# The first transfers in another order, and the empty rows of both expert tables written in eight pieces

## The chip, the core and the metric

The kernel runs on one core of one Trainium2 chip. The core has five engines that run their own instruction streams and meet at semaphores: TensorE (PE, matrix products), VectorE (DVE), ScalarE (ACT), GpSimd (POOL) and SyncE (SP), which here computes nothing and issues nearly all transfers. The metric is the device time of one execution in microseconds (us); lower is better.

## What is computed

The reference is a stack of four residual blocks on x, which is 16 batches of 128 tokens with 128 features, with a condition vector and a context of 77 rows for each batch:

```python
x = x + xcond_0(layernorm(x), cond, ctx)   # adaLN, self-attention, cross-attention, GLU feed-forward
x = x + ffn_0(layernorm(x))                # shared expert + 7 routed experts, top 2
x = x + xcond_1(cond, ctx, layernorm(x))   # slot attention over ctx, 3 rounds
x = x + ffn_1(layernorm(x))                # 8 routed experts, top 1
```

The first block is the one that matters here. For each batch it does

```python
h1 = adaln(x, t, norm1_w, norm1_b);  x = mha(h1, h1, wq, wk, wv, wo) + x        # 16 heads of 64
h2 = adaln(x, t, norm2_w, norm2_b);  x = mha(h2, context, wq2, wk2, wv2, wo2) + x
h3 = adaln(x, t, norm3_w, norm3_b);  x = glu_ff(h3, w1, b1, w2, b2) + x
```

## The kernel before, in words

All arithmetic is float32. The first phase is a software pipeline over the 16 batches, written out by hand for every engine (`iteration(i, S)`, from i = -1 to 17). In iteration i the self-attention of batch i ("A"), the cross-attention of batch i-1 ("B") and the feed-forward and routing of batch i-2 ("C") stand interleaved in twelve steps, with the q, k and v projections of batch i+1 ("N"). The tables `FILL`, `SCORE_STEP`, `SUM_STEP` and `TURN_STEP` set the order within an iteration; each engine executes its stream strictly as written, with waits on semaphores in between.

Before the pipeline come the loads. SP issues them in the order of the code, all on one queue, and the engines wait for them by semaphore:

- `ld_x_first` and `ld_small`: the first two batches of x, condition, adaLN weights, identity, columns (lines 485 to 489).
- `ld_att1` (48): wq, wk, wv of self-attention (line 491), waited for by PE before iteration -1.
- `ld_x`: the other 14 batches of x (line 492, in `load_x` at line 483), waited for by DVE in iteration 0, where the early norms of batches 2 to 5 begin.
- `ld_rows` (48): the row constants, spread to all partitions, the output weights `wo[0]` of self-attention, and the router weights `wr`. POOL waits for all three before it adds a bias row to x (`add_row`, line 1832), and PE before `wo1` of iteration 0 (line 642).
- `ld_ctx`: the context, which PE transposes (line 609) before iteration 0.
- `ld_att2` (64): the q and k weights of cross-attention (`qk2_w`, line 498), its v weights `wv[1]` (line 499) and its output weights `wo[1]` (line 500). PE waits for all four at its first use of any, `v2_0` of iteration 0 (line 633), then makes the products `a2_0` to `a2_3` (line 711).
- `ld_ff`, `ld_moe`, `ld_slot`: what later phases use.

In iteration 0 PE's stream begins with the first two score units of batch 0 (line 652), then `v2_0`, `a2_0`, `a2_1`, `a2_2`, the next two score units (line 652), `q1_1` (line 627) and the transposes of the first softmax (line 677). ACT empties `v2_0` (line 1045) before its first exponential (line 1118); DVE's sums and POOL's scaling (line 1881) follow from that exponential.

The values of cross-attention go through DRAM: SP stores a block of 128 context rows when ACT has emptied it (`store_values`, line 514) and loads the 77 rows of one batch when they are stored and the buffer is free (`load_values`, line 520). `values(i)` does both for batch i. The load for batch b is used by PE at line 689 in iteration b+1, second half.

Two tables in DRAM, `rows_a` (118 regions of 128 rows) and `rows_b` (135 regions), receive the tokens that go to the experts. Their empty rows are written first, by copies of prepared arrays from DRAM to DRAM (line 531), after `values(0)`. POOL waits for `zeroed` before its first scatter of a token row into `rows_a`, in iteration 14.

After the first phase come the shared expert, the routed blocks of table a, slot attention, and the blocks of table b. None of that code is touched.

Of the kernel before, what the change touches and what calls it, by code (L numbers as in the profile page):

```python
# [11 lines left out]
P = 128  # L12
B = 16
# [65 lines left out]
FIRST_TILES = 2  # L79
# [2 lines left out]
LN_STEPS = 3  # L82

SCATTER_FROM = 4

RANK_AT = [last + 3 for _, last in PARTS["a"][:-1]]

# [129 lines left out]
def at(i, count):  # L217

    return count(i)
# [17 lines left out]
def program(nc, A, row_names, out):  # L237
    PLAN = proj_plan()
    with ExitStack() as ctx:
# [9 lines left out]
        def sem(name):  # L249
            return ctx.enter_context(nc.semaphore(name))  # L250
# [133 lines left out]
        def quads(t):  # L384
# [6 lines left out]

        ld_x, ld_small, ld_att1, ld_att2, ld_ff, ld_ctx = (
            sem(n) for n in ("ld_x", "ld_small", "ld_att1", "ld_att2", "ld_ff", "ld_ctx"))
        ld_x_first, ld_rows, rows_added = sem("ld_x_first"), sem("ld_rows"), sem("rows_added")
        pre_dve = sem("pre_dve")
        pre_ada = sem("pre_ada")
# [84 lines left out]
        def _(sp):  # L481
            def load_x(first, last, sem_):
                sp.dma_start(x_sb[:, first:last, :], A["x"][first:last].rearrange("b s d -> s b d")).then_inc(sem_, 16)
# [5 lines left out]
            sp.dma_start(cols[:, :], A["cols"]).then_inc(ld_small, 16)  # L489
            for j in range(3):  # L490
                sp.dma_start(watt[:, 0, j, :], A["att_w"][j]).then_inc(ld_att1, 16)
            load_x(FIRST_TILES, B, ld_x)
            sp.dma_start(rows[:, :], A["rows"].partition_broadcast(P)).then_inc(ld_rows, 16)
            sp.dma_start(ctx_n[:, :, :], A["ctx"].rearrange("b c d -> c b d")).then_inc(ld_ctx, 16)
            sp.dma_start(wo[0], A["att_wo"][0].rearrange("(c p) n -> p c n", p=P)).then_inc(ld_rows, 16)
            sp.dma_start(wr[:, :], A["wr_t"]).then_inc(ld_rows, 16)
            for j in range(2):
                sp.dma_start(qk2_w[:, j, :, :], A["att2_qk"][j].rearrange("(c p) n -> p c n", p=P)).then_inc(ld_att2, 16)
            sp.dma_start(wv[1], A["att_w"][3]).then_inc(ld_att2, 16)
            sp.dma_start(wo[1], A["att_wo"][1].rearrange("(c p) n -> p c n", p=P)).then_inc(ld_att2, 16)  # L500
            sp.dma_start(w1[:, :], A["ff_w1"]).then_inc(ld_ff, 16)
            sp.dma_start(w2[:, :, :], A["ff_w2"].rearrange("(c p) n -> p c n", p=P)).then_inc(ld_ff, 16)
            sp.dma_start(gate_up[:, :], A["gate_up"][EA]).then_inc(ld_moe, 16)
# [21 lines left out]
                    store_values(i)  # L525
                load_values(i)

            values(0)
            sp.wait_ge(consts_ready, 1)
            for t, pad in ((rows_a, A["pad_a"]), (rows_b, A["pad_b"])):  # L530
                sp.dma_start(*(v.rearrange("(p n) d -> p (n d)", p=P) for v in (t, pad))).then_inc(zeroed, 16)
            for i in range(1, B):
                values(i)
            first_phase_over(sp)
            sp.dma_start(cb2[:, :, :].rearrange("p b d -> p (b d)"),
                         A["cond"].rearrange("b d -> (b d)").partition_broadcast(P)).then_inc(ld_cond, 16)
# [58 lines left out]
        def _(pe):  # L595
# [102 lines left out]
            def fill(i, name):  # L698
                half = int(name[-1]) if name[-1] in "01" and "_" in name else 0
                if STREAM[name] == "N" and i == -1:  # L700
                    pe.wait_ge(pre_act, 1)
                if STREAM[name] == "N" and i + 1 in [first for first, _ in X_GROUPS]:
                    emptied_by([first for first, _ in X_GROUPS].index(i + 1), "hT")
                if name.startswith("a2"):
                    if name == "a2_0":
                        pe.wait_ge(ld_att2, 64)
                    t, j = use(i, name), int(name[-1])
                    p = slice(DH * (j % 2), DH * (j % 2) + DH)
                    for h in range(QH):
                        c = 4 * (j // 2) + h  # L710
                        mm = pe.matmul(t[:, h * P:(h + 1) * P], qk2_w[p, 1, c, :], qk2_w[p, 0, c, :], start=True, stop=True)
                    mm.then_inc(proj_full, 1)
                if name.startswith("g2"):
                    if i == 0:
                        emptied_by(i, "a2_3")
                    b, t = i - i % 2, use(i, name)
                    for n, h in enumerate(G2_HEADS[int(name[-1])]):
                        mm = pe.matmul(t[:, n * 2 * C:(n + 1) * 2 * C], a2[:, h, :], ctxT[:, b * C:(b + 2) * C],  # L718
                                       start=True, stop=True)
                    mm.then_inc(proj_full, 1)  # L720
                if name.startswith("v2"):
                    if i == 0:
                        pe.wait_ge(ld_att2, 64)
                    rows_ = slice(P * V2_BLOCK[i], min(P * V2_BLOCK[i] + P, B * C))
                    v_proj(i, name, wv[1], ctxT[:, rows_], half, rows_.stop - rows_.start)
                if name.startswith("q1"):
                    qk_proj(i, name, wq, h1T[:, i + 1, :], half, P)
                if name.startswith("k1"):
                    qk_proj(i, name, wk, h1T[:, i + 1, :], half, P)
                if name.startswith("v1"):  # L730
                    v_proj(i, name, wv[0], h1T[:, i + 1, :], half, P)
                if name == "wo1":
                    if i == 0:
                        pe.wait_ge(ld_rows, 48)
                    pe.wait_ge(o_kept, at(i, lambda t: units_before(t) // 2 + QH // 2))
                    o_proj(i, name, "A", wo[0])
                if name == "wo2":
                    pe.wait_ge(o_kept, at(i, lambda t: units_before(t) // 2))
                    o_proj(i, name, "B", wo[1])
                if name == "hT":  # L740
                    first, last = X_GROUPS[i]
                    t = use(i, name)
                    pe.wait_ge(pre_dve, x_normed(i))
                    for b in range(first, last):
                        mm = pe.transpose(t[:, (b - first) * P:(b - first + 1) * P], z_all[:, b, :], eye[:, :])
                    mm.then_inc(proj_full, 1)
                if name == "h2T":
                    pe.wait_ge(z_ready["A"], i)
                    turn(i, name, zA)
                if name == "h3T":  # L750
                    pe.wait_ge(z_ready["B"], i - 1)
                    turn(i, name, zB)
                if name == "gate":
                    if is_iteration(i, 2):
                        pe.wait_ge(ld_ff, 32)
                    emptied_by(i, "h3T")
                    qk_proj(i, name, w1[:, FF:2 * FF], h3T[:, :], 0, P)
                if name == "lin":
                    qk_proj(i, name, w1[:, 0:FF], h3T[:, :], 0, P)
                if name == "ffout":  # L760
                    t = use(i, name)
                    emptied_by(i, "lin")
                    for c in range(FF // P):
                        mm = pe.matmul(t[:, 0:D], glu[:, c, :], w2[:, c, :], start=(c == 0), stop=(c == FF // P - 1))
                    mm.then_inc(proj_full, 1)
                if name == "zT":
                    pe.wait_ge(z_ready["C"], i - 1)
                    turn(i, name, zC)
                if name == "rank":
                    rank_sums("a", RANK_AT.index(i), use(i, name))  # L770
                if name == "logit":
                    t = use(i, name)
                    emptied_by(i, "zT")
                    pe.matmul(t[:, 0:EA], zT[:, :], wr[:, :], start=True, stop=True).then_inc(proj_full, 1)
# [1032 lines left out]
        def _(pool):  # L1807
# [47 lines left out]
            def early_scatter(i, k):  # L1855

                for part, rank_at in enumerate(RANK_AT):
                    first, last = PARTS["a"][part]
                    if (i, k) == (rank_at, 0):
                        pool.wait_ge(ld_slot, 48)  # L1860
                        for n in range(2):
                            pool.tensor_copy(sent[n][:, first:last, D], tok_ids[:, n, first:last]).then_inc(sent_ready, 1)
                    if (i, k) == (rank_at + 2, SCATTER_FROM):
                        pool.wait_ge(zeroed, 32)
                        pool.wait_ge(routed["a"], part + 1)
                        pool.wait_ge(sent_ready, 2 * part + 2)
                        pool.wait_ge(z_kept, last + 1)
                    n = (N_STEPS - SCATTER_FROM) * (i - rank_at - 2) + k - SCATTER_FROM
                    if k >= SCATTER_FROM and n in range(2 * (last - first)):
                        scatter_one("a", n % 2, first + n // 2)  # L1870
# [178 lines left out]
```

## Time and profile before

| | us |
|---|---|
| median of 3 runs | 942.78 |
| range of the runs | 941.45 to 943.51 |
| span of the profiled execution | 942.8 |
| PE busy in it | 803.7 (85%) |
| DVE busy | 568.8 (60%) |
| ACT busy | 540.2 (57%) |
| POOL busy | 360.0 (38%) |

The profiled execution and the median agree, so its instants can be used as they stand. The page gives busy time by engine, the span in forty slices with TensorE's granted clock, and the groups of instructions with what ended the idle time before them. Other views of the same execution are the timeline (instructions with their start and length), the waits (who waited for whom), the windows (busy time, clock and transfer rate in a stretch), the transfers with their time from issue to landing, and the chain that ended last, followed back through a stretch.

### The profile page before, as it was taken

How to read it: one execution, taken by the hardware profiler on the slowest of the kernel's cores; microseconds unless marked ns; L12 is line 12 of the kernel's file. 1: busy time of each engine (PE TensorE's matmuls, PEld its weight loads, DVE VectorE, ACT ScalarE, POOL GpSimd, SP SyncE). 2: the span in 40 equal slices, each digit the busy share in tenths (PEclk: the TensorE clock that was granted, in tenths of full speed). 3: DMA queues.
4: the chain of work that ended last, by engine and by line, in shares of the span. 5: the costliest groups of instructions: out<-in, count | busy, mean ns of one | idle time of the engine just before them, and what ended most of it. 6: DMA issues, size and time to landing. Idle time of an engine off the chain costs nothing.

```text
span 942.8 us, 18988 instructions
## 1 busy us (share of the span) xinstructions
PE 803.7 (85%) x6173; PEld 673.0 (71%) x6173; DVE 568.8 (60%) x1941; ACT 540.2 (57%) x1147; POOL 360.0 (38%) x559
## 2 busy tenths in 40 slices
PE   5899899999999999999987588999978786861693
PEld 5777787888878888788876456999746565651693
DVE  2576887677866668776575352333558787885012
ACT  2565676667766677666754222333448888851362
POOL 1233454333333333332656150566422222226363
PEclk9897999999999999999998789999855979795697
DMA  9699111001010101000100131888600000001574
GB/s 284 230 314 342 70 37 37 15 1 50 2 37 1 51 1 37 15 1 37 48 27 20 45 105 40 245 249 243 209 7 1 1 0 1 1 1 37 152 208 126
DMA packets 43275, 78.50 MB, mean 83 GB/s; under 512 B 5339, under 2 KB 28587, under 8 KB 42651
## 3 DMA queue, kind: packets, MB, share of 16 engines
q1 hardware_dynamic: 39691, 70.09, 23.8%
q0 software_dynamic: 3488, 7.20, 2.2%
q8 instruction: 52, 0.85, 0.4%
q14 instruction: 44, 0.36, 0.1%
HBM read 63.98 MB, written 30.13 MB: 100 GB/s over the span
## 4 chain that ended last, share of the span: by engine, by line
PE 55%; DVE 20%; issue 9%; POOL 6%; ACT 6%; DMA 2%; SPq 2%; DVEq 0%; ACTq 0%; POOLq 0%
PE bank L899 5%; PE bank L627 5%; PE bank L689 5%; PE bank L652 4%; PE bank L642 3%; DVE sb_smax L1396 3%; PE bank L633 3%; PE bank L677 3%; DVE sb_row_sum L1406 3%; PE bank L907 3%; PE bank L661 3%; PE bank L1008 2%; PE bank L1016 2%; DVE sb_st_all L1704 2%; PE bank L718 2%
## 5 line engine op out<-in xcount | busy, mean ns | idle before, releaser
L1881 POOL TENSOR_TENSOR sb_expd<-sb_expd,sb_rden 128x512 f32<-128x512 f32 (+1 forms) x128 | 112.4, 878 | 259.4 <-DVE sb_rden L1410 259.3
L1396 DVE TENSOR_REDUCE sb_smax<-bank 128x4 f32<-128x512 f32 (+1 forms) x128 | 74.1, 579 | 64.3 <-PE bank L652 39.7
L1973 POOL TENSOR_TENSOR sb_rstd_all<-sb_rsq_all,sb_halves 128x4 f32<-128x4 f32 x44 | 45.2, 1026 | 133.5 <-DVE sb_rsq_all L1711 133.5
L677 PE MATMUL bank<-sb_eye,sb_expd 128*128 128x128 f32 (+1 forms) x512 | 77.5, 278 | 5.7 <-POOL sb_expd L1881 5.2
L1118 ACT ACTIVATE sb_expd<-sb_shifted 128x512 f32<-128x512 f32 (+1 forms) x128 | 69.8, 545 | 18.9 <-DVE sb_shifted L1399 17.9
L677 PEld LDWEIGHTS bank<-sb_eye,sb_expd 128*128 128x128 f32 (+1 forms) x512 | 59.7, 145 | 26.8 <-issue 13.5
L1406 DVE TENSOR_REDUCE sb_row_sum<-sb_expd 128x4 f32<-128x512 f32 (+1 forms) x128 | 73.0, 570 | 9.4 <-ACT sb_expd L1118 9.4
L1112 ACT ACTIVATE sb_probT<-bank 128x512 f32<-128x512 f32 (+1 forms) x128 | 74.3, 590 | 7.2 <-PE bank L677 6.9
L1399 DVE TENSOR_TENSOR sb_shifted<-bank,sb_smax 128x512 f32<-128x512 f32 (+1 forms) x128 | 75.0, 586 | 4.4
L627 PE MATMUL bank<-sb_h1T,sb_watt 128*128 128x128 f32 x512 | 72.1, 287 | 4.7 <-DMA sb_watt<-att_w 2.3
L689 PE MATMUL bank<-sb_probT,sb_v 128*64 128x128 f32 (+1 forms) x1024 | 71.7, 283 | 5.0 <-issue 3.4
L627 PEld LDWEIGHTS bank<-sb_h1T,sb_watt 128*128 128x128 f32 x512 | 64.1, 198 | 9.5 <-DVE sb_xb L1385 3.7
L689 PEld LDWEIGHTS bank<-sb_probT,sb_v 128*64 128x64 f32 (+1 forms) x1024 | 56.1, 139 | 14.7 <-issue 4.7
L899 PE MATMUL bank<-sb_blk_xT,sb_up_w 128*128 128x128 f32 x456 | 57.1, 275 | 0.0
L1939 POOL DMA_INDIRECT back_a<-sb_blk_y,sb_dest_a x38 | 37.0, 973 | 48.7 <-issue 24.9
L899 PEld LDWEIGHTS bank<-sb_blk_xT,sb_up_w 128*128 128x128 f32 x456 | 54.0, 192 | 0.0
L1671 DVE TENSOR_TENSOR sb_hid<-bank,sb_hid 128x384 f32<-128x384 f32 x38 | 21.2, 558 | 51.1 <-ACT sb_hid L1167 51.1
L661 PE MATMUL bank<-sb_g,sb_h2T 128*128 128x308 f32 x128 | 48.4, 460 | 0.0
L1201 ACT ACTIVATE sb_z_all<-sb_S,sb_nbias,sb_rstd_all 128x128 f32<-128x128 f32 x96 | 39.3, 482 | 10.6 <-DVE sb_nbias L1717 10.3
L1167 ACT ACTIVATE sb_hid<-bank 128x384 f32<-128x384 f32 x38 | 18.6, 491 | 40.6 <-PE bank L899 40.6
L652 PE MATMUL bank<-sb_k1T,sb_q1T 64*128 64x128 f32 x512 | 38.2, 289 | 3.6 <-DVE sb_shifted L1399 3.1
L718 PEld LDWEIGHTS bank<-sb_ctxT,sb_watt 128*128 128x128 f32 x256 | 36.8, 190 | 4.6 <-issue 2.4
(256 smaller groups left out, 1917.2 us busy)
## 6 DMA issues: line engine op xcount, KB each, us to landing
sb_up_w<-gate_up SPq DMA_DIRECT2D x38, 384.0 KB
rows_b<-pad_b SPq DMA_DIRECT2D x1, 8775.0 KB, 53.6
rows_a<-pad_a SPq DMA_DIRECT2D x1, 7670.0 KB, 27.9
sb_up_w<-w1b SPq DMA_DIRECT2D x23, 256.0 KB
sb_v<-v_all SPq DMA_DIRECT2D x16, 308.0 KB
v_all<-sb_v_rows SPq DMA_DIRECT2D x9, 512.0 KB, 2.6
sb_blk_x<-rows_a SPq DMA_DIRECT2D x38, 65.0 KB, 3.3
sb_watt<-att_w SPq DMA_DIRECT2D x4, 512.0 KB, 6.3
```

What stands on the lines that cost most here:

```text
L627: mm = pe.matmul(t[:, c * n:(c + 1) * n], w[:, (4 * half + c) * P:(4 * half + c + 1) * P], src, start=True, stop=True)
L652: mm = pe.matmul(score[(u + r) % 2][:, h, :], q1T[p, 4 * (j // 2) + h, :], k1T[p, 4 * (j // 2) + h, :], start=True, stop=True)
L661: pe.matmul(score[u % 2][:, :, 0:C], h2T[:, :], g2[:, QH * j:QH * (j + 1), first:first + C], start=True, stop=True).then_inc(score_done, 1)
L677: mm = pe.transpose(trans[u % 2][0:n, h, :], expd[:, (units_before(i) + u) % EXP_RING, h, 0:n], eye[:, :])
L689: mm = pe.matmul(pvo[DH * r:DH * r + DH, h, :], v[:, 8 * (j // 2) + 2 * h + r, :], probT[0:n, (u - 1 + r) % 2, h, :], start=True, stop=True)
L899: mm = pe.matmul(bank[1 + 2 * j + v][:, c * P:(c + 1) * P], up_w[:, (u + 1) % NSLOT, (j * CA + c) * P:(j * CA + c + 1) * P], blk_xT[:, v, ...
L1112: act.activation(probT[0:n, u % 2, :, :], trans[u % 2][0:n, :, :], ACT.Copy).then_inc(probT_ready, 1)
L1118: act.activation(expd[:, (units_before(i) + u) % EXP_RING, :, 0:n], shifted[:, u % 2, :, 0:n], ACT.Exp, scale=DH ** -0.5).then_inc(exp_don ...
L1396: dve.tensor_reduce(smax[:, u % 2, :], s_in, X, ALU.max).then_inc(max_done, 1)
L1399: dve.tensor_tensor(shifted[:, u % 2, :, 0:n], s_in, smax[:, u % 2, :].unsqueeze(2).broadcast_to([P, QH, n]), ALU.subtract).then_inc(sub_d ...
L1406: dve.tensor_reduce(row_sum[:, u % 2, :], expd[:, (units_before(i) + u) % EXP_RING, :, 0:n], X, ALU.add).then_inc(row_sum_done, 1)
L1881: pool.tensor_tensor(e, e, rden[:, u % 2, :].unsqueeze(2).broadcast_to([P, QH, n]), ALU.mult).then_inc(norm_done, 1)
```

## The change

Six lines of loads change places. The context, the v weights of cross-attention and its q and k weights now follow the self-attention weights at once; the row constants, `wo[0]` and `wr` come after them, then the 14 batches of x. The output weights `wo[1]` get a semaphore of their own, `ld_wo2`, and PE waits for that at `wo2` of iteration 2; the two waits for `ld_att2` count 48 instead of 64. The empty rows of the tables are no longer written by two copies after `values(0)`, but by eight pairs of copies, one pair after each of `values(1)` to `values(8)`. POOL's wait for `zeroed` counts 256 instead of 32.

```diff
+PAD_PARTS = 8
...
+        ld_wo2 = sem("ld_wo2")
...
             for j in range(3):
                 sp.dma_start(watt[:, 0, j, :], A["att_w"][j]).then_inc(ld_att1, 16)
-            load_x(FIRST_TILES, B, ld_x)
+            sp.dma_start(ctx_n[:, :, :], A["ctx"].rearrange("b c d -> c b d")).then_inc(ld_ctx, 16)
+            sp.dma_start(wv[1], A["att_w"][3]).then_inc(ld_att2, 16)
+            for j in range(2):
+                sp.dma_start(qk2_w[:, j, :, :], A["att2_qk"][j].rearrange("(c p) n -> p c n", p=P)).then_inc(ld_att2, 16)
             sp.dma_start(rows[:, :], A["rows"].partition_broadcast(P)).then_inc(ld_rows, 16)
-            sp.dma_start(ctx_n[:, :, :], A["ctx"].rearrange("b c d -> c b d")).then_inc(ld_ctx, 16)
             sp.dma_start(wo[0], A["att_wo"][0].rearrange("(c p) n -> p c n", p=P)).then_inc(ld_rows, 16)
             sp.dma_start(wr[:, :], A["wr_t"]).then_inc(ld_rows, 16)
-            for j in range(2):
-                sp.dma_start(qk2_w[:, j, :, :], A["att2_qk"][j].rearrange("(c p) n -> p c n", p=P)).then_inc(ld_att2, 16)
-            sp.dma_start(wv[1], A["att_w"][3]).then_inc(ld_att2, 16)
-            sp.dma_start(wo[1], A["att_wo"][1].rearrange("(c p) n -> p c n", p=P)).then_inc(ld_att2, 16)
+            load_x(FIRST_TILES, B, ld_x)
+            sp.dma_start(wo[1], A["att_wo"][1].rearrange("(c p) n -> p c n", p=P)).then_inc(ld_wo2, 16)
...
-            values(0)
-            sp.wait_ge(consts_ready, 1)
-            for t, pad in ((rows_a, A["pad_a"]), (rows_b, A["pad_b"])):
-                sp.dma_start(*(v.rearrange("(p n) d -> p (n d)", p=P) for v in (t, pad))).then_inc(zeroed, 16)
-            for i in range(1, B):
+            def empty_rows(n):
+                for t, pad, x in ((rows_a, A["pad_a"], "a"), (rows_b, A["pad_b"], "b")):
+                    each = -(-NREG[x] // PAD_PARTS)
+                    part = slice(P * each * n, P * min(each * (n + 1), NREG[x]))
+                    sp.dma_start(*(v[part, :].rearrange("(p n) d -> p (n d)", p=P) for v in (t, pad))).then_inc(zeroed, 16)
+
+            for i in range(B):
                 values(i)
+                if 1 <= i <= PAD_PARTS:
+                    empty_rows(i - 1)
...
-                        pe.wait_ge(ld_att2, 64)
+                        pe.wait_ge(ld_att2, 48)
...
+                    if is_iteration(i, 2):
+                        pe.wait_ge(ld_wo2, 16)
...
-                        pool.wait_ge(zeroed, 32)
+                        pool.wait_ge(zeroed, 32 * PAD_PARTS)
```

On SP, the first loads. Before, from the self-attention weights to the feed-forward's (`att_wo` stands twice, for `wo[0]` and then for `wo[1]`; `sb_g2<-att2_qk` is `qk2_w`, which shares its tile):

```order
L491 DMA sb_watt<-att_w 128x1024 x3
L483 DMA sb_x<-x 128x14x128
L493 DMA sb_rows<-rows 128x1245
L494 DMA sb_ctx<-ctx 77x16x128
L495 DMA sb_watt<-att_wo 128x8x128
L496 DMA sb_wr<-wr_t 128x7
L498 DMA sb_g2<-att2_qk 128x8x128 x2
L499 DMA sb_watt<-att_w 128x1024
L500 DMA sb_watt<-att_wo 128x8x128
```

And now:

```order
L495 DMA sb_watt<-att_w 128x1024 x3
L496 DMA sb_ctx<-ctx 77x16x128
L497 DMA sb_watt<-att_w 128x1024
L499 DMA sb_g2<-att2_qk 128x8x128 x2
L500 DMA sb_rows<-rows 128x1245
L501 DMA sb_watt<-att_wo 128x8x128
L502 DMA sb_wr<-wr_t 128x7
L487 DMA sb_x<-x 128x14x128
L504 DMA sb_watt<-att_wo 128x8x128
```

Four transfers moved ahead of the row constants, and x moved from the first place to the last but one. `wo[1]` stands where it stood.

Further on in SP's stream, after the loads, stand the copies of the empty rows among the stores (`v2_all<-`) and loads (`sb_v2<-`) of values. Before:

```order
L514 DMA v2_all<-sb_v2_rows 128x1024 [waits proj_act]
L520 DMA sb_v2<-v2_all 77x1024 [waits v2_stored]
L531 DMA rows_a<-pad_a 128x15340 [waits consts_ready]
L531 DMA rows_b<-pad_b 144x15600
L514 DMA v2_all<-sb_v2_rows 128x1024 [waits proj_act]
L520 DMA sb_v2<-v2_all 77x1024 [waits v2_stored]
L520 DMA sb_v2<-v2_all 77x1024 [waits pv_done,v2_stored]
```

And now:

```order
L518 DMA v2_all<-sb_v2_rows 128x1024 [waits proj_act]
L524 DMA sb_v2<-v2_all 77x1024 [waits v2_stored]
L518 DMA v2_all<-sb_v2_rows 128x1024 [waits proj_act]
L524 DMA sb_v2<-v2_all 77x1024 [waits v2_stored]
L536 DMA rows_a<-pad_a 16x15600
L536 DMA rows_b<-pad_b 32x8840
L524 DMA sb_v2<-v2_all 77x1024 [waits pv_done,v2_stored]
L536 DMA rows_a<-pad_a 16x15600
L536 DMA rows_b<-pad_b 32x8840
```

The first pair of copies now stands behind the store and load for batch 1, and the next pair behind the load for batch 2; six more pairs follow in the same way. The streams of PE, DVE, ACT and POOL keep their instructions in their places.

## Rows read from the trace of the kernel before

**Rows 1.** The page: the clock granted to TensorE in forty slices of the span, tenths.

```profile
PEclk9897999999999999999998789999855979795697
```

**Rows 2.** The waits of 15 to 33 us: who waited for whom, total, times, longest.

```profile
PE bank L633 <- DMA sb_watt<-att_wo: 3.5, 1, 3.5
```

**Rows 3.** The chain of 19 to 32 us: start us, us, what.

```profile
26.02 2.07 PE bank L633 x2
28.09 2.91 PE bank L711 x23
```

**Rows 4.** The timeline of 15 to 33 us: start, us, instruction [idle before <-releaser].

```profile
19.42 0.72 POOL L1832 TENSOR_TENSOR sb_x0b<-sb_x0b,sb_rows 128x256 f32<-128x256 f32 x1 [12.28 <-DMA sb_wr<-wr_t]
...
21.41 1.16 PE L652 MATMUL bank<-sb_k1T,sb_q1T 64*128 64x128 f32 x16 [0.52 <-ACT sb_ctxT L1031]
...
24.65 0.69 DVE L1399 TENSOR_TENSOR sb_shifted<-bank,sb_smax 128x512 f32<-128x512 f32 x1
...
28.62 0.62 ACT L1118 ACTIVATE sb_expd<-sb_shifted 128x512 f32<-128x512 f32 x1
...
30.26 1.04 POOL L1881 TENSOR_TENSOR sb_expd<-sb_expd,sb_rden 128x512 f32<-128x512 f32 x1 [9.43 <-DVE sb_rden L1410]
...
32.93 0.27 PE L677 MATMUL bank<-sb_eye,sb_expd 128*128 128x128 f32 x1
```

**Rows 5.** Transfers issued in 5 to 18 us: KB each, us from issue to landing.

```profile
sb_rows<-rows SPq DMA_DIRECT2D x1, 622.5 KB, 10.7
...
sb_watt<-att_wo SPq DMA_DIRECT2D x1, 512.0 KB, 8.4
...
sb_wr<-wr_t SPq DMA_DIRECT2D x1, 3.5 KB, 6.1
...
sb_g<-att_qk SPq DMA_DIRECT2D x1, 512.0 KB, 6.4
sb_watt<-att_w SPq DMA_DIRECT2D x1, 512.0 KB, 6.6
```

**Rows 6.** Windows: stretch, length, PE busy (instructions), granted clock, DMA share, GB/s.

```profile
19.00:23.00 4.00, 2.58 (x33) 1.00 1.07 348
23.00:26.00 3.00, 0.00 (x0) 0.50 1.09 378
26.00:29.80 3.80, 3.78 (x13) 0.50 1.08 436
70.00:74.00 4.00, 2.48 (x30) 1.00 0.89 296
76.00:84.80 8.80, 8.80 (x50) 0.52 1.01 335
108.00:112.00 4.00, 2.36 (x13) 1.00 0.00 0
```

**Rows 7.** The chain at full clock, at 38 us and at 112 to 119 us.

```profile
38.91 1.06 PE bank L633 x2
...
112.60 1.02 PE bank L689 x16
...
116.68 1.78 PE bank L642 x16
```

**Rows 8.** The chain at half clock, in 74 to 90 us.

```profile
78.72 1.91 PE bank L689 x16
```

**Rows 9.** The page: the second copy of empty rows, KB, us from issue to landing.

```profile
rows_b<-pad_b SPq DMA_DIRECT2D x1, 8775.0 KB, 53.6
```

**Rows 10.** The timeline at four places: DVE's, SP's, PE's and POOL's.

```profile
38.99 0.84 DVE L1270 BATCH_NORM_STATS2 sb_st_all<-sb_x 128x6 f32<-128x128 f32 x4
...
100.18 0.73 SPq L520 DMA_DIRECT2D sb_v<-v_all  x2
...
106.56 1.09 PE L689 MATMUL bank<-sb_probT,sb_v 77*64 77x128 f32 x16 [0.53 <-issue]
...
455.49 1.20 POOL L1851 DMA_INDIRECT rows_a<-sb_sent,sb_slot  x1 [0.18 <-issue]
```

More of the change, by code:

```diff
@@ L722, in fill @@
                     if i == 0:
-                        pe.wait_ge(ld_att2, 64)
+                        pe.wait_ge(ld_att2, 48)
                     rows_ = slice(P * V2_BLOCK[i], min(P * V2_BLOCK[i] + P, B * C))
```

## Prediction

> **What bounds the kernel now.** I read the page first, for the clock: it dips twice in the first four of forty slices [rows 1]. Then the waits of the opening, since the change is there: between 15 and 33 us PE waits for one transfer, 3.5 us [rows 2], and POOL for another, 12.3 us [rows 4]. The chain says which of the two counts: it runs through PE's `v2_0` (line 633) and the 24 products at line 711 behind it [rows 3], and ahead of them through the output weights of cross-attention; POOL's wait isn't on it. PE had finished the first score units at 21.41 + 1.16 = 22.57 us [rows 4] and started `v2_0` at 26.02 [rows 3]. The other engines have nothing on the path in between: DVE is done with both shifted scores at 24.65 + 0.69 = 25.34, and ACT's first exponential at 28.62 stands behind the emptying of `v2_0` [rows 4]. So in this stretch the landing of a transfer is the bound. The rest of the first phase goes by PE, DVE and the clock, whose code the change leaves alone.
>
> **The stall goes: -3.45 us.** PE waits for 64 counts of `ld_att2`. The last of them come from `wo[1]`, which `v2_0` doesn't read. Now 48 are enough, and their three transfers stand early. When do they land? The queue is the limit, its engines being full (share 1.07 [rows 6]), and transfers land about in the order of issue. Before, 896 + 622.5 + 616 + 512 + 3.5 = 2650 KB went between the self-attention weights and the end of `wr`, which landed when POOL resumed, at 19.4 [rows 4]. Now the context, wv and qk2 are 616 + 512 + 1024 = 2152 KB. By bytes I put them between the row constants (1518.5 KB, issued at 5.11, landed at 15.8) and `wo[0]` (2646 KB, 10.57 + 8.4 = 19.0) [rows 5]: 15.8 + 3.2 x 633/1128 = 17.6 us. The bounds are 15.8 and 19.4, and both lie before 22.57, the later one by 3.2 us. So the whole wait goes: 26.02 - 22.57 = 3.45.
>
> **The clock behind the stall: 0 to -1.25 us.** The clock fell to half (1.2 of 2.4 GHz) at 23.0, 0.4 us after PE went idle, and rose at 29.8, after 3.8 us of unbroken work [rows 6]. Under it `v2_0` took 2.07, against 1.06 for the same two instructions at full clock [rows 3, 7], and the 24 products took 2.91 [rows 3]; at the full-clock rate of line 642, 1.78/16 = 0.111 each [rows 7], they take 2.67. Together 1.01 + 0.24 = 1.25. Without the stall PE works on through the instant of the fall. The trace can't say whether the clock then stays: in the 4 us ahead of the fall PE was busy for 2.58, and the change adds only 0.4. But 108 to 112 us, with 2.36 of 4, saw no fall [rows 6], so such a share doesn't force one. I take it that it stays, the fall having come once PE stood still. If it falls at 23.0 all the same, PE does the same work at half clock, and the term is near 0.
>
> The Trainium skill, "TensorE: Matmul & The Clock Gate", Part 1, says that the gate's window is free-running and doesn't reset when a kernel starts. By that rule either end of this term can come up from run to run, 938.1 or 939.3. No row here shows it, since there is one profile.
>
> **What is late next.** From 22.57 on, PE ends `v2_0` at 23.6 and the 24 products at 26.3. The second score units need DVE's second subtraction, 25.34 [rows 4], which is early by 1. ACT empties `v2_0` at 23.7 and does the exponential at 24.3; POOL then scales 4.3 us earlier than its 30.26 [rows 4], at 25.9 to 27.0. The transposes at line 677, 32.93 before [rows 4], come at 28.2 in PE's order, 1.2 us after their input. PE stays last, so the shift of 4.7 arrives whole.
>
> **Loads that moved back: 0.** The row constants, `wo[0]` and `wr` now end at 3290 KB. Before, 2650 had landed at 19.4 and 3674, through qk2, at 16.59 + 6.4 = 23.0 [rows 5], which gives 21.6. POOL adds its two rows in 1.45 us, so it is through at 23.0 and at worst at 24.5; its next work is at 25.9, and that idle time is the cover. If it were gone, POOL's first scaling would be late by what is over, with 1.2 us to spare ahead of PE. PE uses `wo[0]` only behind the transposes of 28.2. x ends where wv ended, with the same bytes ahead of it: 17.88 + 6.6 = 24.5 [rows 5]; DVE first reads it at 38.99 [rows 10], some 34 now. `wo[1]` stands in its old place, landed at 26.0 [rows 3], and is used in iteration 2, behind 78.7 [rows 8]. PE's new wait costs nothing.
>
> **The empty rows in pieces: 0.** Before, 16.4 MB stood in the queue from 45 us on, and the second copy took 53.6 us to land [rows 9], at 99. The store of values for batch 1 sat behind them, so the load went out only at 100.18 [rows 10]. PE used it at 106.56, and its idle 0.53 there ends 0.1 us after ACT's last turned probabilities [rows 10]; the load wasn't late. So the pieces win nothing on the chain. Nor would the load have become late through the opening's gain, since the copies start behind `values(0)` and move with it. SP now issues 16 copies at 0.6 to 0.7 us each in an idle stream, each pair behind the load of `values(i)`. What is queued behind the last pieces is the next store of values, and at the rate of before a pair takes 53.6/8 = 6.7 us, against 13 us or more to the next thing that SP issues. The last pair goes out near 275 us; POOL asks for `zeroed` just before 455.5 [rows 10].
>
> **The sum.** 942.8 - 3.45 - 1.25 = **938.1 us**, made against the profiled execution, whose span equals the median.
>
> **The rivals.** *The clock falls at 23.0 anyway.* Only the stall goes: 942.8 - 3.45 = 939.3. For it speaks that PE's share before the instant, 2.58 of 4, is about that before the other fall, 2.48 of 4 at 70 to 74 us [rows 6].
>
> *The second dip goes as well.* From 74 to 85 us the clock is at half while PE is busy throughout, 8.8 of 8.8 us in 76 to 84.8 [rows 6]. Line 689 took 1.91 there against 1.02 at full clock [rows 7, 8], a factor of 1.87; 8.8 - 8.8/1.87 = 4.1 us, so 934.0. Against it: the thin stretch before that fall is made by DVE's instructions of iteration 1, which move along with everything else.
>
> *A new dip.* All that follows moves by 4.7 us, and a thin stretch such as 108 to 112 us may meet a fall where it met none. Priced as the second dip, one gives 938.1 + 4.1 = 942.2, no change. Two give 946.3; slower begins between the two.
>
> *The pieces land too late.* The copies have 16 and 32 rows now, 128 and 144 before. Should so few rows be carried by few of the 16 engines, a pair takes longer: with one engine 16 x 6.7 = 107 us, and eight of them from 60 us on end at 916, 460 us past POOL's wait, so 1400 us. It decides from (455 - 60)/8 = 49 us a pair, which is 2 engines or fewer. For it speaks only the new shape; against it, that there are as many rows as engines and that a row is as long as one of before (15600 elements).
>
> The Trainium skill, "DMA: Bandwidth & Descriptors", section on why a DMA increments its semaphore by 16, says that such a transfer goes over the largest number of engines, up to 16, that divides its slowest dimension. By that rule the pieces use all 16 and take the 6.7 us.
>
> **Chances.** Forecast, 938.1: 0.40. Fall at 23.0 anyway, 939.3: 0.22. Second dip gone, with or without the first, about 934.0: 0.22. One new dip, 942.2: 0.10. Slower, by two dips or late pieces: 0.06. The runs spread by 1 us to either side of the median, and so does each case. The range must leave out no more than 2 in 10: 933.3 to 941.0 holds the first two cases whole, some five sixths of the third and a tenth of the fourth, 0.40 + 0.22 + 0.18 + 0.01 = 0.81. A difference of 0.2%, 1.9 us, is about what a measurement of this kernel can tell from none. Below 940.9 lie the first three cases and a little of the fourth: 0.85. Within 0.2%: 0.09. Slower: 0.06.
>
> **What would show it.** PE goes from line 652 to `v2_0` at 22.6 without a wait for a transfer; POOL's `add_row` stands near 21.6, the transposes at line 677 near 28.2, and everything to 70 us is 4.7 us early. The clock at 23 us tells the forecast from the first rival, and the clock between 70 and 85 the second. Stores of values land within 3 us, and pairs of copies in 7. The forecast is wrong if `ld_att2` is still waited for after 22.6, if ACT or POOL becomes the late input of line 677, or if the gain of the opening is there at 70 us and is gone at 943.

## The result and the profile after

| | before | after |
|---|---|---|
| median, us | 943.14 (6 runs) | 936.44 (6 runs) |
| range, us | 941.45 to 947.19 | 932.87 to 938.01 |
| profiled execution: time, span | -, 942.8 | 932.87, 931.1 |

The ratio of after to before is 0.9916, with a 95% interval of 0.9891 to 0.9940: 7.9 us faster, by the interval between 5.7 and 10.3. The forecast was 938.1, in a range of 933.3 to 941.0. The profiled execution of after happens to be the fastest of its six, 3.6 us below their median, so its span says less than where in it the time went.

**The opening.** The chain of waits of the changed kernel, 21 to 29 us (start us, us, what). Its lines 617, 635, 641, 660, 685 and 719 are 609, 627, 633, 652, 677 and 711 of before.

```profile
21.61 1.16 PE bank L660 x16
22.78 1.05 PE bank L641 x2
23.83 2.08 PE bank L719 x23
...
26.02 0.89 PE bank L660 x15
26.92 1.09 PE bank L635 x8
28.01 0.44 PE bank L685 x4
```

No transfer stands in it any more. PE goes from the score units (line 660) to `v2_0` (line 641) at 22.78, where it stood still until 26.02 before [rows 3]; there `v2_0` takes 1.05 and not 2.07, the first 23 of the 24 instructions at line 719 take 2.08 and not 2.91 [rows 3], and the transposes come at 27.84 instead of 32.93 [rows 4] (the chain, which shows only what PE did last, has them from 28.01). The timeline shows what the prediction named beside PE: POOL's `add_row`, and its first scaling.

```profile
22.18 0.72 POOL L1842 TENSOR_TENSOR sb_x0b<-sb_x0b,sb_rows 128x256 f32<-128x256 f32 x1 [14.91 <-DMA sb_wr<-wr_t]
...
26.43 1.04 POOL L1891 TENSOR_TENSOR sb_expd<-sb_expd,sb_rden 128x512 f32<-128x512 f32 x1 [2.84 <-DVE sb_rden L1420]
...
27.84 0.60 PE L685 MATMUL bank<-sb_eye,sb_expd 128*128 128x128 f32 x4
```

**The clock.** The page's row of the clock in forty slices, and windows of the changed kernel (stretch, length, busy us and instructions of PE, PE's weight loads, DVE, ACT and POOL, granted clock, DMA share, GB/s).

```profile
PEclk9999999999999999999998689999956979795797
```

```profile
22.70:26.00 3.30, 3.30 (x33) 2.54 (x33) 3.13 (x5) 2.13 (x4) 0.89 (x2) 1.00 1.07 334
70.00:74.00 4.00, 3.34 (x35) 2.31 (x36) 1.09 (x5) 3.17 (x7) 1.68 (x3) 1.00 0.02 4
76.00:84.80 8.80, 7.94 (x79) 7.07 (x78) 7.24 (x17) 5.78 (x11) 3.33 (x4) 1.00 0.39 158
100.00:104.80 4.80, 3.77 (x13) 2.29 (x15) 2.76 (x12) 2.76 (x8) 2.59 (x6) 0.64 0.00 0
```

Both dips of the first slices [rows 1] are gone: the clock is 1.00 where it was 0.50 and 0.52 [rows 6]. A short new one, 3.4 us at half clock from 101.2, is in the last window. The copies of empty rows land in 6.4 and 8.5 us each, the stores of values in 2.6, by the page:

```profile
rows_b<-pad_b SPq DMA_DIRECT2D x7, 1105.0 KB, 8.5
rows_a<-pad_a SPq DMA_DIRECT2D x7, 975.0 KB, 6.4
...
v_all<-sb_v_rows SPq DMA_DIRECT2D x9, 512.0 KB, 2.6
```

**How much earlier, and where.** I matched PE's instructions in two traces and took the difference of their starts. The changed kernel runs 5.1 us ahead of before at 40 and 70 us, 8.2 at 97, 7.8 from 135 to 670, and 11.9 at 920. So the opening gives 5.1, the missing second dip 3.1, the stretch with the new one takes 0.4, and the last phase, whose code is the same, gives 4.1. What of this belongs to the change, and what to the one execution that was profiled, is what the experiments are for.

### The profile page after: what moved, and what is told of

The parts are those of the page before. It is cut to its first block, busy times and chain, and to the rows that moved or that the text cites. A ratio compares the mean times of both kernels' runs of the same rounds, so it can differ in the third digit from the quotient of the medians.

```text
span 931.1 us, 19002 instructions
## 1 busy us (share of the span) xinstructions
PE 796.0 (85%) x6173; PEld 666.3 (72%) x6173; DVE 568.6 (61%) x1941; ACT 540.7 (58%) x1147; POOL 360.9 (39%) x559
## 4 chain that ended last, share of the span: by engine, by line
PE 56%; DVE 21%; issue 8%; ACT 6%; POOL 6%; DMA 2%; DVEq 0%; SPq 0%; ACTq 0%; POOLq 0%
PE bank L635 6%; PE bank L909 5%; PE bank L697 5%; PE bank L660 4%; PE bank L650 3%; DVE sb_smax L1406 3%; PE bank L641 3%; PE bank L685 3%; PE bank L669 3%; PE bank L917 3%; DVE sb_row_sum L1416 3%; PE bank L1018 2%; DVE sb_st_all L1714 2%; PE bank L726 2%; PE bank L1026 2%
## 5 line engine op out<-in xcount | busy, mean ns | idle before, releaser
L1211 ACT ACTIVATE sb_z_all<-sb_S,sb_nbias,sb_rstd_all 128x128 f32<-128x128 f32 x96 | 39.3, 481 | 10.8 <-DVE sb_nbias L1727 10.4
```

## The experiments

The same lead over the first profile of before, in us, at the instants 40, 97, 135 and 920 of that profile (negative: later). "New" and "old" loads are those of after and of before. The ratio is to runs of the kernel before on the same chip.

| kernel | median us (runs) | ratio, 95% interval | lead at 40 | 97 | 135 | 920 |
|---|---|---|---|---|---|---|
| after | 936.44 (6) | 0.9916 [0.9891, 0.9940] | 5.1 | 8.2 | 7.8 | 11.9 |
| e6: after again | 934.48 (6) | 0.9892 [0.9866, 0.9919] | 5.0 | 8.2 | 8.2 | 11.4 |
| e5: before again | 946.38 (12) | 1.0009 [0.9986, 1.0031] | -2.2 | 0.9 | -0.8 | 1.1 |
| e1: new loads alone | 937.58 (5) | 0.9896 [0.9871, 0.9921] | 5.9 | 9.1 | 7.4 | 5.1 |
| e10: the same again | 940.34 (5) | 0.9900 [0.9863, 0.9938] | 5.8 | 8.9 | 4.8 | 4.4 |
| e2: pieces alone | 942.04 (9) | 0.9953 [0.9930, 0.9976] | -2.3 | 0.9 | 0.5 | 5.0 |
| e7: the same again | 944.05 (12) | 0.9996 [0.9973, 1.0019] | -2.2 | 1.0 | 1.0 | 0.3 |
| e3: old order, `wo[1]` apart | 941.97 (6) | 0.9926 [0.9899, 0.9953] | -1.2 | 1.4 | 1.5 | -0.6 |
| e4: before, stall filled | 945.13 (11) | 0.9986 [0.9960, 1.0012] | -1.6 | 1.0 | 1.0 | -1.0 |
| e9: after, stall put back | 943.64 (7) | 0.9958 [0.9932, 0.9984] | -2.4 | 0.2 | 0.2 | 0.8 |
| e11: that stall filled | 939.79 (6) | 0.9934 [0.9910, 0.9959] | 1.4 | 4.5 | 4.5 | 8.1 |
| e12: whole copies, later | 933.91 (6) | 0.9895 [0.9872, 0.9918] | 4.7 | 7.8 | 7.5 | 10.4 |
| e8: pieces on two engines | 1005.15 (2) | 1.0644 [1.0598, 1.0690] | 4.5 | 7.7 | 7.7 | -62.5 |

### The two parts alone

New loads alone (e1) is the changed kernel with the two whole copies in their old place; pieces alone (e2) is its complement. e1 against after:

```diff
...
-            for i in range(B):
+            values(0)
+            sp.wait_ge(consts_ready, 1)
+            for t, pad in ((rows_a, A["pad_a"]), (rows_b, A["pad_b"])):
+                sp.dma_start(*(v.rearrange("(p n) d -> p (n d)", p=P) for v in (t, pad))).then_inc(zeroed, 16)
+            for i in range(1, B):
                 values(i)
-                if 1 <= i <= PAD_PARTS:
-                    empty_rows(i - 1)
...
-                        pool.wait_ge(zeroed, 32 * PAD_PARTS)
+                        pool.wait_ge(zeroed, 32)
```

> The loads in their new order with wo[1] on its own semaphore; the empty rows as before, in two copies after values(0). Theory: the opening's gain comes from the loads alone, so the first transposes at the line that was 677 stand 5.1 us earlier than before (28.0), and the time is that of the changed kernel within 2 us, ratio 0.991 to 0.995; the value load for batch 1 still waits for the copies, lands near 98 us, and is not late by more than 1 us at its use near 98 to 101. Rival (the pieces bring part of the gain): ratio 0.996 or more, and the clock's dip near 74 us stays, since the copies' traffic stays.

> The loads as before, the empty rows in eight pairs. Theory: ratio 0.998 to 1.002, the stall at v2_0 of 3.45 us and both dips of the clock (23 and 74 us) as in the kernel before. Rival (the traffic of the copies has to do with the dip at 74 us, which is gone in the changed kernel): no dip there, ratio near 0.996.

Measured: 0.9896 and 0.9953. The loads bring the whole gain, and in the medians a little more than was expected of them (a ratio of 0.991 at the lowest). One expectation for e1 failed: the load for batch 1 came 2.5 us late for PE, not 1 at the most (more on this under "The pieces, or their place"). The pieces' ratio of 0.9953 didn't come back when the same kernel ran again (0.9996, below), so alone they are worth 0 to 0.5%.

### The old order with `wo[1]` on a semaphore of its own, and the stall filled

e3 keeps the order of the loads and only frees `v2_0` from `wo[1]`:

```diff
-            sp.dma_start(wo[1], ...).then_inc(ld_att2, 16)
+            sp.dma_start(wo[1], ...).then_inc(ld_wo2, 16)
...
-                        pe.wait_ge(ld_att2, 64)
+                        pe.wait_ge(ld_att2, 48)
...
+                    if is_iteration(i, 2):
+                        pe.wait_ge(ld_wo2, 16)
```

> Only wo[1] gets a semaphore of its own; order of the loads and the empty rows as before. PE then waits for wv alone, which landed at 24.5 us: the stall shrinks from 3.45 to 1.9 us. Theory: gain 1.5 us plus what the clock does, ratio 0.997 to 0.999. If the order were idle and the semaphore the whole effect, the ratio would be that of the changed kernel, 0.992.

The chain of e3, 19 to 34 us:

```profile
18.46 6.17 DMA sb_watt<-att_w
24.63 0.04 issue
24.68 2.07 PE bank L637 x2
26.75 3.83 PE bank L715 x23
```

wv[1] is now the late transfer, and PE waits 1.7 us by the waits. The clock falls at 23.6 all the same, now for 10.2 us, so line 715 (711 in before) takes 3.83: at 40 us this kernel is 1.2 behind the profile of before, with half of its stall gone. But its ratio, 0.9926, with an interval of 0.9899 to 0.9953, isn't the 0.997 to 0.999 of my theory; it is what I expected if the semaphore were the whole effect. The profiled execution was the slowest of the six (945.01 us, the fastest 936.34), so its trace may not stand for the others. By the traces the new order adds 6.3 us at 40 us to what the semaphore brings (5.1 against -1.2); by the medians how much it adds isn't shown.

e4 leaves the wait where it is and lets PE work in it:

```diff
+                    if i == 0 and name == "v2_0":
+                        for _ in range(7):
+                            pe.matmul(use(i, name)[:, :], eye[:, :], wq[:, 0:512], start=True, stop=True)
                     if i == 0:
                         pe.wait_ge(ld_att2, 64)
```

> The kernel before with 7 products of 128x512 put on PE ahead of v2_0 (their result is overwritten by v2_0), so that PE stands idle no more while it waits; nothing else differs. v2_0 then starts near 26.3 instead of 26.0. Theory: the clock does not fall at 23 us, v2_0 and the 24 products take 3.1 us instead of 5.0, and the transposes stand 1.5 us earlier than before; this is the clock's share of the opening's gain. Rival (the fall at 23.0 is due to what came before it): it falls all the same, and the kernel is slower by 0.3 us or more.

The chain of e4, 22 to 33 us:

```profile
23.44 6.21 PE bank L724 x14
29.65 0.86 PE bank L633 x2
30.51 2.08 PE bank L711 x23
```

The seven products took 6.21 us, not the 3.5 of the stall, and pushed `v2_0` from 26.02 to 29.65, where 26.3 was expected. But the clock stayed at full until 75 us, and of these 3.6 us only 1.6 are left at 40 us: the other 2.0 are what the kernel before loses at half clock behind its stall. The filling overshot, so the pair e9 and e11 asks the same with a shorter one.

### Before, after and the pieces again

> The kernel before, unchanged, for a second profile and for the spread of a ratio that must be 1. Theory: the dips of the clock lie elsewhere than in the first profile, since they come at instants of their own and meet the program at another place; the opening's dip lasts 6.8 or 10.2 us, the dip near 74 us lasts 0 to 10.2 us; ratio 0.998 to 1.002. Rival (the dips belong to the code): both as in the first profile.

> The changed kernel, unchanged, for a second profile. Theory: no stall at v2_0 and no dip before 30 us again, with the opening 5 to 6 us shorter than in the kernel before; the later dips lie elsewhere than in the first profile, so the gain behind 470 us is between -2 and +4 us; ratio 0.990 to 0.994. Rival (the pieces bring 3 us of it): ratio lower than that of the loads alone, 0.9896, by 0.002 or more.

> The pieces alone once more; their first ratio, 0.9953, was lower than the theory's 0.998. Theory (the pieces bring nothing, the first ratio was the clock's luck): 0.998 to 1.001, and stall and dip at 23 us as before. Rival (the pieces bring 2 to 4 us, by the clock or by transfers in 45 to 99 us): 0.993 to 0.997.

The second profile of before (e5) is the most instructive trace of all. Its chain, 19 to 34 us and 100 to 112 us:

```profile
26.15 2.08 PE bank L633 x2
28.22 3.83 PE bank L711 x23
...
104.74 3.43 DMA sb_v<-v_all
108.17 0.04 issue
108.21 1.09 PE bank L689 x16
```

Three things differ from the first. The opening dip lasts 10.2 us instead of 6.8, and the lead falls to -2.2. There is no dip at 74 us, which gives 3.1 back. And then PE waits 3.1 us for the values of batch 1, at 105, which costs 1.8 of lead. The sum is -0.8: two executions within 1 us of each other that spend their time differently. e6 repeats after within 0.4 us in every column up to 135.

### The stall put back

e9 is the changed kernel with one wait more; e11 is e9 with three products in the wait.

```diff
                     if i == 0:
                         pe.wait_ge(ld_att2, 48)
+                        pe.wait_ge(ld_wo2, 16)
```

```diff
+                    if i == 0 and name == "v2_0":
+                        for _ in range(3):
+                            pe.matmul(use(i, name)[:, :], eye[:, :], wq[:, 0:512], start=True, stop=True)
```

> The changed kernel, with one wait more: v2_0 waits for wo[1] again, as before the change. PE is ready for it at 22.7 us; wo[1] is issued at 17.2 and its landing took 7.3, so v2_0 should start at 24.5 to 25.5, a stall of 1.8 to 2.8 us. Theory (what makes the half clock of the opening is PE standing still before v2_0, not the order of the loads): the clock falls at 23 to 24 us for 6.8 to 13.7 us, the 24 products take 2.9 to 3.8 instead of 2.1, everything at 45 to 70 us is 5 to 8 us later than in the changed kernel, ratio to the kernel before 0.997 to 1.002. Rival (the fall belongs to the old order, or to chance): no fall, the lag against the changed kernel is the stall alone, 2 to 3 us, ratio 0.992 to 0.994.

> The kernel with the stall put back, and in the stall three products of 128 by 512 of the identity with wq, written into the bank that v2_0 writes over anew: 0.9 us each, so 2.7 us of work where PE would stand still. Theory (idle makes the fall): no half clock between 22 and 45 us, v2_0 at 25.4 to 26, everything at 45 to 70 us later than in the changed kernel by the 2.7 to 3 us of the delay alone, less what was slack; ratio 0.992 to 0.995, so faster than the kernel with the empty stall although v2_0 starts no earlier. Rival: the clock falls as in the empty stall, same time as that one or later.

The chain of e9, and then that of e11, 20 to 34 us:

```profile
20.77 1.16 PE bank L660 x16
21.93 3.85 issue
25.78 2.04 PE bank L641 x2
27.83 3.83 PE bank L719 x23
```

```profile
22.95 2.77 PE bank L732 x6
25.72 0.73 issue
26.45 1.10 PE bank L641 x2
27.55 2.08 PE bank L719 x23
```

The chain calls the wait of e9 "issue", without naming the transfer. With PE idle for 3.85 us the clock falls (at 24.9 us, for 10.2) and line 719 costs 3.83; at 40 us e9 is 7.5 us behind after, 3.0 of them from the later start of `v2_0`, which leaves 4.5 for work at half clock. With PE busy in the same wait `v2_0` starts 0.7 us later still, nothing runs at half clock, and at 40 us e11 is 3.7 behind after: only its later start. The ratios stand in the same order, 0.9958, 0.9934, and 0.9916 and 0.9892 without the wait, though the intervals of e9 and e11 overlap and each has one trace. So it isn't the order of the loads that holds the clock here; it is that PE doesn't stand still before `v2_0`.

One profile doesn't fit this account. In e7 the clock fell at 21.1 us, 1.7 us before PE's wait for `wo[1]` began, while PE worked on the first score units (stretch, length, PE busy and instructions, granted clock, DMA share, GB/s):

```profile
18.12:18.57 0.45, 0.00 (x0) 1.00 0.89 262
18.57:21.10 2.53, 1.76 (x18) 1.00 1.02 295
21.10:22.84 1.74, 1.74 (x16) 0.50 1.13 382
```

There the score units already take 1.94 us instead of 1.16. The 0.45 us at 18.12 is a wait for the context, which also stood behind other loads in the old order. Whether that wait brought the fall wasn't tried.

### The pieces, or their place

e10 repeats the new loads alone:

> The new order of loads with the old two copies of empty rows, a second time. Theory (the pieces are worth nothing): the same ratio as the changed kernel within the interval, 0.988 to 0.992, and no half clock ahead of 95 us. Rival (the pieces bring about 2 us by thinner traffic behind 45 us): 0.993 to 0.995.

The waits of 90 to 115 us, of e1 and then of e10 (who waited for whom, total, times, longest):

```profile
PE bank L693 <- DMA sb_v<-v_all: 2.5, 1, 2.5
```

```profile
PE bank L693 <- DMA sb_v<-v_all: 4.5, 1, 4.5
```

and the chain of e10, 56 to 104 us:

```profile
56.44 41.59 DMA v_all<-sb_v_rows
98.02 0.02 issue
98.04 3.55 DMA sb_v<-v_all
101.59 0.04 issue
101.63 1.97 PE bank L693 x16
```

The store of 512 KB, issued at 56.44, lands 41.6 us later behind the empty rows. PE is ahead by 8.9 us, but the load goes out only 2.1 us earlier than in before (98.04 against 100.18 [rows 10]), though the copies went out 4.9 earlier. Of the 6.8 us between the two, the load's spare time in before takes up some 3, and the rest is the wait of 4.5, with the 0.5 that PE stood idle there anyway [rows 10]. The time from the issue of the first copy to that of the load isn't the same in every execution either: 55.5 us in the first profile of before, the shortest, 56.2 to 57.3 in e3, e1, e4 and e5, and 58.3 in e10. Between 97 and 135 us e1 loses 1.7 us and e10 4.1; after and e6, with pieces, lose 0.4 and 0.0. e12 asks whether that is the work of the pieces or of their place: two whole copies, behind the load for batch 2.

```diff
...
             for i in range(B):
                 values(i)
-                if 1 <= i <= PAD_PARTS:
-                    empty_rows(i - 1)
+                if i == 2:
+                    for t, pad in ((rows_a, A["pad_a"]), (rows_b, A["pad_b"])):
+                        sp.dma_start(*(v.rearrange("(p n) d -> p (n d)", p=P) for v in (t, pad))).then_inc(zeroed, 16)
...
-                        pool.wait_ge(zeroed, 32 * PAD_PARTS)
+                        pool.wait_ge(zeroed, 32)
```

> The new order of loads, with the two copies of empty rows whole, but issued behind the load of values for batch 2 (near 74 us) and no longer behind that for batch 0 (near 39 us). With the copies in their old place and the new loads, PE waited 2.5 and 4.5 us near 101 us for the values of batch 1, which stood in the queue behind them. Theory (it is the place in the queue that makes this wait, not the size of the copies): PE has no wait for a load of values between 90 and 115 us, the next store of values, issued near 120, lands behind the copies at 128 to 131 and its load is in at 134, ahead of its use at 161; PE keeps 8 us of lead over the kernel before from 95 to 470 us, as with eight pieces; ratio 0.988 to 0.992, span 931 to 934. Rival (only pieces help; whole copies slow whatever moves beside them or make the next values late): a wait of PE for values between 120 and 165 us, lead down to 4 to 6 us, ratio 0.993 or more.

SP's timeline in e12, 55 to 135 us:

```profile
74.17 0.68 SPq L536 DMA_DIRECT2D rows_a<-pad_a  x1
74.89 0.58 SPq L536 DMA_DIRECT2D rows_b<-pad_b  x1
120.45 0.35 SPq L518 DMA_DIRECT2D v_all<-sb_v_rows  x1
130.41 0.29 SPq L524 DMA_DIRECT2D sb_v<-v_all  x1
```

The next store takes 10 us and not 2.6, but its values are used only near 161, and PE waits for none. The lead goes from 7.8 to 7.5, as in after, and the ratio is 0.9895. So the place in the queue makes the wait, and two copies in a better place do what sixteen do. This rests on the traces: the ratios of e1 and e10, which have the wait, are no worse (0.9896 and 0.9900).

### The pieces on two engines

To give the rival of late pieces its case, e8 leads each copy by a dimension of 2:

```diff
-                    sp.dma_start(*(v[part, :].rearrange("(p n) d -> p (n d)", p=P) for v in (t, pad))).then_inc(zeroed, 16)
+                    rows_of = 16 if x == "a" else 32
+                    m = (part.stop - part.start) * ROW // rows_of
+                    sp.dma_start(*(v[part, :].rearrange("r d -> (r d)").rearrange("(a b m) -> b a m", b=2, m=m)
+                                   for v in (t, pad))).then_inc(zeroed, 16)
```

> The changed kernel with each copy of empty rows led by a dimension of 2, the rows as long as before. The page on transfers says that 2 engines then carry it. Theory (that rule holds): a pair lands after 8 x 6.7 = 54 us instead of 7, eight pairs from 60 us on end near 490, POOL waits for them near 450, and the time is 30 to 45 us longer, 965 to 980. Rival (rows are spread over all engines whatever leads): a pair lands in 7 to 9 us and the time is that of the changed kernel.

Its window of 125 to 145 us (columns as above), SP's timeline there, and the waits of 90 to 360 us:

```profile
125.00:145.00 20.00, 17.29 (x151) 13.85 (x149) 11.45 (x37) 10.08 (x19) 6.03 (x11) 1.00 0.12 50
```

```profile
120.24 0.35 SPq L518 DMA_DIRECT2D v_all<-sb_v_rows  x1
144.93 0.29 SPq L524 DMA_DIRECT2D sb_v<-v_all  x1
```

```profile
ACT sb_v_rows L1058 <- DMA v_all<-sb_v_rows: 37.7, 2, 31.6
...
PE bank L638 <- ACT sb_v_rows L1058: 28.6, 1, 28.6
...
PE bank L700 <- DMA sb_v<-v_all: 27.8, 3, 13.4
```

A DMA share of 0.12 is 2 of 16 engines. Two pairs, issued from 60.65 on, are through near 144, 42 us each, where the longer copy of a pair took 8.5 in after. 42 is less than the 54 expected and less than the 49 from which I let the rival decide. Yet e8 takes 71 us more than the changed kernel on the same chip (1005.15 against 934.48 in e6), not 30 to 45, because it strikes elsewhere: ACT can't empty the next block of values while the store of the last block is in the queue, PE waits 28.6 us for ACT, and another 27.8 for its values.

## Why the prediction came out as it did

**The stall goes.** Right in every step: no wait for a transfer, `add_row` at 22.18 (21.6 forecast), the transposes at 27.84 (28.2), PE last throughout, and the loads that moved back cost nothing. `v2_0` starts 3.24 us earlier (22.78 for 26.02), not 3.45, since PE itself came to it 0.2 later.

**The clock behind the stall.** The direction was right, and it was the likeliest case, but two terms were too small. The 24 "products" of the prediction are 24 instructions, two to a product; 23 of them take 2.08 at full clock in every trace that has it. I priced the 24 at 2.67 by line 642, which starts one every 0.111 us. A single group of eight at line 719 keeps that pace too (`a2_3` in after, from 30.16 us, one every 0.112). But `a2_0`, `a2_1` and `a2_2` use the two halves of 64 rows in turn, and where one follows another their instructions start in pairs, 0.004 to 0.006 us apart. I overlooked that overlap. So against the first profile alone the term is 1.02 + 0.83 = 1.85, not 1.25. And the bound of 1.25 came from one dip of 6.8 us. In e5, e2, e3 and e9 it lasts 10.2, in e7 13.7, and line 719 then costs 3.83. Against e5 the opening gives 7.3 us, and e9 puts 4.5 of its 7.5 down to the clock. By these profiles this is the main part of what the measured 7.9 has over the forecast 4.7; for the executions that weren't profiled it isn't shown.

**The clock falls at 23 anyway.** Refuted: in all six profiles that have the new loads and no wait (after, e1, e6, e8, e10, e12), and in both with the wait filled, it stays at full until after 70 us; in all six with the idle wait (before, e2, e3, e5, e7, e9) it falls, in five of them after PE had gone idle and in e7 before. The Trainium skill's rule ("TensorE: Matmul & The Clock Gate", Part 1, a free-running window) would have let either case come up from run to run. The start and the length of the dip did vary so, 21.1 to 24.9 us and 6.8 to 13.7; its presence did not.

**The second dip gone.** It came true in the profile, 3.1 us rather than 4.1, and proved nothing about the change: e5, the kernel before, has none either, and e3, e4 and e9 have one of 3.4 us. It is a matter of the execution. My sum was made against the one trace that has it in this length.

**The empty rows: 0.** In the first trace the load wasn't late, by some 3 us. The step that failed is the one after it: "nor would the load have become late through the opening's gain, since the copies start behind `values(0)` and move with it". They move with it, but the second dip stood between them and PE's use of the load, and hid the wait; and the first profile also had the shortest time from the copies to the load, 55.5 us. Without that dip PE waits 3.1 us in e5, 1.7 in e3 and 1.4 in e4 for those values, and 2.5 and 4.5 with the new loads. What it costs is 0 to 4.1, since in e3 and e4 the lead doesn't change. The medians can't tell it: 0.9896 and 0.9900 without the pieces, 0.9916 and 0.9892 with them.

**Pieces too late.** Not so with 16 and 32 rows: 6.4 and 8.5 us a copy, so that a pair is through some 9 us after its first issue; the 6.7 I took for it was too short, but nobody was waiting. That the pieces go over all the engines agrees with the rule of the Trainium skill ("DMA: Bandwidth & Descriptors", on why a DMA increments its semaphore by 16), as e8's share of 0.12 does for a dimension of 2. The threshold of 49 us was mis-sized: I looked at the last consumer, POOL, and not at the next transfers behind each pair.

**The base.** The result's times are 1.8 us above their spans (932.87 and 931.1), so the profiled 942.8 of before is a time of 944.6, and not the median of 942.78 that I set it equal to. With that base the sum is 939.9, and misses the measured 936.44 by 3.5. That 938.1 came within 1.7 is partly luck: the base was too low and the gain too small, and in the forecast time the two errors work against each other.

**What stays open.** From 450 to 920 us the lead changes by +4.1 in after and -2.3 in e1, +4.5 in e2 and -0.7 in e7, with the same code there. The clock's dips of the last phase fall otherwise from execution to execution (slices 22 to 40 of the page's row); why they differ wasn't tried. Nor is it settled why e3's ratio, 0.9926, is better than its trace, or why the clock fell in e7 before the wait.

## What to carry to other kernels

A stall of PE can be paid twice: for its own length, and again for what runs behind it at half clock; filling the wait with throw-away products recovered most of the second part, 3.8 us of 7.5 here, and moving the transfer recovers both. Large copies without a reader belong behind the small transfers that somebody will wait for soon. As to how they are cut, two whole copies did as well as sixteen pieces, but pieces that went over 2 engines cost 71 us. And a single profile can hide a late transfer behind a dip of the clock: profile the kernel before twice before pricing a wait at nothing.

## What the runs showed of the hardware

- With a wait of PE of 1.7 to 4.5 us before `v2_0`, the half-clock stretch lasted 6.8, 10.2 or 13.7 us in different executions; the longest wait (e2, 4.5 us) didn't have the longest stretch.
- Instructions of 64 rows and 128 columns (line 719) start every 0.112 us at full clock and every 0.213 at half, as long as one group runs by itself. Where a group on the other half of the rows follows, the two overlap: 23 take 2.08 us at full clock and 3.83 at half. A product of 128 by 512 takes 0.92 us (2.77/3), as two instructions.
- SP itself can be held by an issue. In after that of `wo[1]` took 4.4 us, by its timeline, against 0.4 for `wo[0]`, of the same size; the transfer engines were full both times, and what makes the difference isn't shown:

```profile
14.78 0.43 SPq L501 DMA_DIRECT2D sb_watt<-att_wo  x1
...
17.22 4.37 SPq L504 DMA_DIRECT2D sb_watt<-att_wo  x1
```
